# Attention, routing and experts on one core: two head units at a time on TensorE, quarter-tile work of both and then full-tile work of both

## The reference, cut to what matters

```python
h = layernorm(x) * (1 + ca) + sa
q, k, v = split(h @ Wqkv)                       # x is (2, 2048, 256); 16 heads of 64
scores = (q @ k.T) * 64 ** -0.5                 # masked to the 128 keys up to the query's own
x = x + ga * ((softmax(scores) @ v) @ Wout)
h = layernorm(x) * (1 + cb) + sb
x = x + gb * moe(h)                             # 8 experts, 2 of them per token, at most 640 tokens per expert and choice
```

## Time and profile before

| what | value |
|---|---|
| median of 3 runs | 1118.7 us (1117.24 to 1118.92) |
| the profiled execution, its own time | 1115.21 us |
| its span, first to last instruction | 1113.4 us |
| TensorE busy | 1050.8 us, 94% of the span |
| TensorE weight loads | 727.3 us, 65% |
| VectorE busy | 780.6 us, 70% |
| ScalarE busy | 660.1 us, 59% |
| GpSimd busy | 498.8 us, 45% |
| granted TensorE clock, mean | 0.986 |

### The profile page before, as it was taken

How to read it: one execution, slowest core, us unless ns; L and a number is a source line. 1 busy time by engine, 2 the same in 40 slices (tenths; PEclk the granted TensorE clock), 3 DMA queues, 4 the chain that set the end, 5 groups by cost and what they waited for, 6 DMA issues and landing times.

```text
span 1113.4 us, 28021 instructions
## 1 busy us (share of the span) xinstructions
PE 1050.8 (94%) x10746; PEld 727.3 (65%) x10746; DVE 780.6 (70%) x1745; ACT 660.1 (59%) x1930; POOL 498.8 (45%) x547
## 2 busy tenths in 40 slices
PE   7989999999999999999989866999999999999995
PEld 3456766766666666666666544668685858586765
DVE  5677767778788787776778864656676666766653
ACT  4677667567667666676655735545547372737460
POOL 2244345456365364554554653533525252435342
PEclk9999999999999999999999998999999999999998
DMA  9654111121121031122121034552535253535000
GB/s 321 121 163 158 32 21 35 44 66 38 37 75 38 9 85 26 24 69 65 43 56 58 21 112 108 101 134 79 122 111 105 95 106 115 105 116 87 15 21 10
DMA packets 140173, 87.59 MB, mean 79 GB/s; under 512 B 96756, under 2 KB 130698, under 8 KB 139916
## 3 DMA queue, kind: packets, MB, share of 16 engines
q1 hardware_dynamic: 129292, 64.29, 22.7%
q0 software_dynamic: 10752, 21.54, 7.2%
HBM read 40.02 MB, written 33.79 MB: 66 GB/s over the span
## 4 chain that ended last, share of the span: by engine, by line
PE 85%; ACT 5%; issue 4%; DVE 3%; POOL 2%; DMA 0%; SPq 0%; ACTq 0%; DVEq 0%
PE down L1838 19%; PE up L1824 17%; PE gen L666 14%; PE gen L786 8%; PE score L703 7%; PE gen L680 6%; PE gen L713 6%; PE pv L745 4%; ACT prob L1029 2%; PE pv L735 2%; DVE prob L1251 1%; ACT norm_space L1053 1%; POOL slot_inputs L1647 1%; ACT hid L1866 1%; DVE negmax L1243 1%
## 5 line engine op out<-in xcount | busy, mean ns | idle before, releaser
L1866 ACT ACTIVATE hid<-up,b1T 128x512 f16<-128x512 f32 (+2 forms) x192 | 124.5, 648 | 182.1 <-PE up L1824 180.4
L1824 PE MATMUL up<-xT,w 128*128 128x512 f16 (+2 forms) x1152 | 212.5, 345 | 11.3 <-issue 11.3
L1636 POOL TENSOR_SCALAR_AFFINE_SELECT probT_split<-probT_split 128x512 f32<-128x512 f32 x128 | 114.3, 893 | 237.7 <-ACT probT_split L1038 237.4
L1838 PE MATMUL down<-w,hid 128*128 128x256 f16 x1920 | 213.7, 274 | 3.2 <-DVE hid L1882 3.2
L1838 PEld LDWEIGHTS down<-w,hid 128*128 128x128 f16 x1920 | 188.4, 98 | 27.8 <-DVE hid L1882 3.7
L666 PE MATMUL gen<-hT,big 128*128 128x512 f16 x768 | 187.0, 383 | 2.8 <-ACT probT_split L1038 2.2
L1029 ACT ACTIVATE prob<-score,negmax 128x128 f32<-128x128 f32 x512 | 180.9, 374 | 2.8 <-DVE negmax L1243 2.8
L1824 PEld LDWEIGHTS up<-xT,w 128*128 128x128 f16 x1152 | 113.0, 98 | 105.3 <-issue 13.3
L1925 POOL DMA_INDIRECT out<-y,tail x80 | 82.5, 1031 | 206.1 <-DVE y L1910 193.2
L1882 DVE TENSOR_TENSOR hid<-hid 128x512 f16<-128x512 f32 (+2 forms) x192 | 115.2, 606 | 72.8 <-ACT hid L1867 72.4
L666 PEld LDWEIGHTS gen<-hT,big 128*128 128x128 f16 x768 | 74.9, 99 | 84.0 <-ACT probT_split L1038 4.8
(11 more groups left out here) (168 smaller groups left out, 1650.1 us busy)
## 6 DMA issues: line engine op xcount, KB each, us to landing
big<-in_L_ffn_W SPq DMA_DIRECT2D x14, 1024.0 KB, 6.5
slot_inputs<-empty_row SPq DMA_DIRECT2D x80, 129.5 KB, 2.5
out<-x SPq DMA_DIRECT2D x7, 512.0 KB
k<-k SPq DMA_DIRECT2D x48, 64.0 KB, 1.8
x<-in_L_attn_x SPq DMA_DIRECT2D x4, 512.0 KB, 4.3
x<-in_L_attn_x SPq DMA_DIRECT2D x2, 1024.0 KB, 14.5
kept<-out,tail POOLq DMA_INDIRECT x80, 3.1
out<-y,tail POOLq DMA_INDIRECT x80, 2.4
```

What stands on the lines that cost most here:

```text
L1636: pool.affine_select(out=own, in_=whole, pattern=[[0, TILES], [-1, P]], compare_op=ALU.is_gt, fill=zero, base=0, channel_multiplier=1).the ...
L1824: mm = pe.matmul(bank, w1[:, par, kd, a, ft * P:(ft + 1) * P], part_rows(e, n, xT[:, par, b * KD + kd, :]), start=(i == 0), stop=(i == 5))
L1838: mm = pe.matmul(down[n][:, s, :], hid[:, ft, a, t * P:(t + 1) * P], w2[:, par, ft, b, :], start=(i == 0), stop=(i == 3 * FT - 1))
L1866: act.activation(part_rows(e, n, hid[:, ft, 0, :]), bank, ACT.Relu, scale=1 / W_SCALE, bias=bias).then_inc(hid_hi, 1)
```

## The change

TensorE now walks the steps in pairs (i, i+1) with i even. It does `scores(i)`, `half_values` of step i, `scores(i+1)`, `half_values` of step i+1, and then the transposes and the rest of step i, and the transposes and the rest of step i+1. ACT walks the same pairs in a new order. In DVE's order three small things move: an output tile's gating goes behind the softmax work of its step, layernorm's normalising goes to step 4 of the next chunk, and the steps after it move by one. The second half of the routing statistics comes at step 11 (was 13), and what follows it comes earlier too; POOL's wait for the sent rows is replaced by waits at the two places that need it. The fourth output tile is made in step 10 (was 12). The first seven chunks are changed; the last chunk keeps its own loop.

```diff
-            OUT_TILE = {4: 0, 6: 1, 8: 2, 12: 3}
+            OUT_TILE = {4: 0, 6: 1, 8: 2, 10: 3}
-            ROUTE_AT = {"stats": (7, 13), "rstd": 14, "norm": 14, "scale": 16, "shift": 17, "token": 18, "pack": 18, "low": (18, 19)}
+            ROUTE_AT = {"stats": (7, 11), "rstd": 12, "norm": 13, "scale": 15, "shift": 16, "token": 17, "pack": 17, "low": 18}
-            LN_STATS, LN_AGGR, LN_RSTD, LN_NORM = 12, 16, 17, (18, 19)
-            LN_SCALE, LN_SHIFT, LN_PACK, LN_LOW = 4, 6, 8, 9
+            LN_STATS, LN_AGGR, LN_RSTD = 16, 18, 19
+            LN_NORM, LN_SCALE, LN_SHIFT, LN_PACK, LN_LOW = 4, 5, 7, 9, 10
...
+            def places_seen(eng, r):
+                if r < NC:
+                    at_least(eng, sent, 16 * TILES * K * (r - 1))
...
 # TensorE
-                        for i in STEPS:
-                            scores(c, i)
-                            half_values(c, i - HI_AT, (c, i - LO_AT) if i >= LO_AT else (c - 1, H - 1) if c > 0 else None)
-                            transposes(H * c + i - 2, c, ("pt", i))
-                            ...
+                        for i in STEPS[::2]:
+                            for n in (i, i + 1):
+                                scores(c, n)
+                                half_values(c, n - HI_AT, (c, n - LO_AT) if n >= LO_AT else (c - 1, H - 1) if c > 0 else None)
+                            for n in (i, i + 1):
+                                rest_of_step(c, n)
...
 # ACT
+                    def evacuations(c, i):
+                        if c > 0 and i in SECOND_V:
+                            values(c - 1, ("v", 1, SECOND_V[i]))
+                        for name in projections_at(c, i):
+                            if name[0] == "v":
+                                evacuate(c, name)
+                    def evacuate_qk(c, i):
+                        for name in projections_at(c, i):
+                            if name[0] != "v":
+                                evacuate(c, name)
...
-                        for i in STEPS:
+                        for i in STEPS[::2]:
                             exponentials(c, i - 1)
+                            if i > LAG:
+                                evacuate_qk(c, i - 1)
+                            elif c > 0:
+                                evacuate_qk(c - 1, STEPS[-1])
                             if i >= LO_AT:
                                 attn_high_part(c, i - LO_AT)
                             elif c > 0:
                                 attn_high_part(c - 1, H - 1)
+                            exponentials(c, i)
+                            attn_high_part(c, i + 1 - LO_AT)
                             copy_probT(c, i - 2)
-                            ...
+                            evacuations(c, i)
+                            evacuate_qk(c, i)
+                            copy_probT(c, i - 1)
+                            evacuations(c, i + 1)
...
 # DVE
-                            if c > 0 and i - 1 in OUT_TILE:
-                                gate_tile(c - 1, OUT_TILE[i - 1])
...
                             if c > 0 and i - 1 in OUT_TILE:
+                                gate_tile(c - 1, OUT_TILE[i - 1])
                                 add_tile(c - 1, OUT_TILE[i - 1])
...
+                                if i == LN_NORM:
+                                    ln_norm(c + 2)
...
 # POOL
-                            if c > 1 and i == pick["sent"]:
-                                pool.wait_ge(sent, 16 * TILES * K * (c - 1))
```

More of the change, by code:

```diff
@@ L402, in route_group @@
                 return (r, kind) if r < NC else (LAST, (kind[0] + "_part", r - NC))
+            def places_seen(eng, r):
+                if r < NC:
+                    at_least(eng, sent, 16 * TILES * K * (r - 1))
             def rows_seen(eng, r):
                 if r < LAST:
[L407 to L412 removed]
+                    places_seen(eng, r)
             def route_scale(eng, r):
@@ L421, in route_shift, with route_low @@
                 eng.tensor_tensor(h2[:], h2[:], modrow[:, batch(r - 1), 1:2, :].to_broadcast([P, TILES, D]), ALU.add).then_inc(r_h2, 1)
-            def route_low(eng, r, half=None):
+            def route_low(eng, r):
                 c, t0, nt, rows_out = route_round(r)
                 eng.wait_ge(r_pack_hi, r)
-                tiles = slice(t0, t0 + nt) if half is None else slice(2 * half, 2 * half + 2)
-                op = eng.tensor_tensor(rows_out[:, tiles, D:2 * D], h2[:, tiles], rows_out[:, tiles, 0:D], ALU.subtract)
-                if half != 0:
-                    op.then_inc(r_pack, 1)
+                eng.tensor_tensor(rows_out[:, t0:t0 + nt, D:2 * D], h2[:, t0:t0 + nt], rows_out[:, t0:t0 + nt, 0:D], ALU.subtract)\
+                   .then_inc(r_pack, 1)
             def load_inputs(sp):
@@ L867, in project, with rest_of_step @@
                             project_qk(cc, name)
-                    def chunk(c):
-                        for i in STEPS:
-                            scores(c, i)
-                            half_values(c, i - HI_AT, (c, i - LO_AT) if i >= LO_AT else (c - 1, H - 1) if c > 0 else None)
-                            transposes(H * c + i - 2, c, ("pt", i))
-                            if c > 0 and i in OUT_TILE:
-                                late_out(c - 1, OUT_TILE[i])
-                            if c > 0 and i in SECOND_V:
-                                project_v(c - 1, 1, [SECOND_V[i]])
-                            for name in projections_at(c, i):
-                                project(c, name)
-                            if c > 1 and i == CHOOSE_AT["logits"]:
-                                route_logits(c - 1)
-                            if c > 1 and i == CHOOSE_AT["counts"]:
-                                route_counts(c - 1)
+                    def rest_of_step(c, i):
+                        transposes(H * c + i - 2, c, ("pt", i))
+                        if c > 0 and i in OUT_TILE:
+                            late_out(c - 1, OUT_TILE[i])
+                        if c > 0 and i in SECOND_V:
+                            project_v(c - 1, 1, [SECOND_V[i]])
+                        for name in projections_at(c, i):
+                            project(c, name)
+                        if c > 1 and i == CHOOSE_AT["logits"]:
+                            route_logits(c - 1)
+                        if c > 1 and i == CHOOSE_AT["counts"]:
+                            route_counts(c - 1)
+                    def chunk(c):
+                        for i in STEPS[::2]:
[4 more added lines that the diff above has]
+                                rest_of_step(c, n)
                         if c == LAST - 1:
@@ L1199, in ln_aggregate, with ln_norm @@
                         op.then_inc(ln_mv, 1)
-                    def ln_norm(cn, tiles=range(TILES)):
+                    def ln_norm(cn):
                         if cn > 2:
                             dve.wait_ge(ln_lo, cn)
-                        norm_rows(dve, x_at(cn), xn, meanvar[0], rstd[0], ln_rstd, ln_xn, cn + 1, tiles)
+                        norm_rows(dve, x_at(cn), xn, meanvar[0], rstd[0], ln_rstd, ln_xn, cn + 1)
                     def ln_scale(cn):
@@ L1490, in chunk @@
                                     ln_aggregate(c + 3)
-                                if i in LN_NORM:
-                                    half = LN_NORM.index(i)
-                                    ln_norm(c + 3, range(2 * half, 2 * half + 2))
                         if c == LAST - 1:
@@ L1657, in chunk @@
                                 reciprocal_std(pool, meanvar[1], rstd[1], r_mv, r_var, r_rstd, c, mv_n=stats_before(c) + 2)
-                            if c > 0 and i in at["low"]:
-                                route_low(pool, c, at["low"].index(i))
+                            if c > 0 and i == at["low"]:
+                                route_low(pool, c)
                             if i == LN_LOW and c + 2 < NC:
@@ L1679, in last_chunk @@
                                 scatter(c - 1, *LAST_SENDS[i])
-                            if i == LAST_SENT:
-                                pool.wait_ge(sent, 16 * TILES * K * (c - 1))
                             if i == at["low"]:
```

21 lines of the change are left out of this document (7 added, 14 removed).

## The result

The changed kernel takes 1242.2 us (median of 4 runs, 1240.9 to 1245.6); the kernel before took 1118.0 beside it (4 runs). The ratio is 1.112, with a 95% interval of 1.110 to 1.114: 124 us slower. The forecast was 1234, with 1168 to 1268 as its range.

A forecast was written before the change was run, and what follows sets the result against it. The prediction took TensorE's own sequence, busy 94% of the span, as the bound. Its terms, 76 + 42 + 18 + 4 - 13 - 7 - 2 = 118 us on 1115.2, gave 1233, stated as 1234 us, range 1168 to 1268.

The forecast's parts named there:

- Wait A: TensorE's values of step i+1 wait for the pv bank until VectorE's `attn_low_part`: 1.36 us in 56 pairs, 76 us.
- Wait B: TensorE's second transposes wait for the gen bank until ScalarE's `probT` copy: 1.40 us in 30 pairs, 42 us.
- Wait C: TensorE's group after the second transposes waits for ScalarE to empty step i's q: 0.5 us 36 times, 18 us.
- The savings: One entry into quarter tiles and one return fewer per pair on TensorE: 0.24 us a pair, 13 us in all.
- The moves and the smaller parts: VectorE late after moved normalising and routing, 4 us; TensorE's earlier waits gone, minus 7; scatters, sent-row wait, SP's work, 0.
- chunk 6: Its last two pairs, with almost no full-tile work, were not bound by TensorE before: 2 us off Wait A.
- its own range: Forecast's narrower range, 1205 to 1262 us: Wait A at 1.1 to 1.6 us, Wait B and Wait C at 70% to all.
- Only wait A: Rival, 20%: the copy or the exponentials come earlier than laid out, so only the pv bank wait costs: 1175 us.
- The savings alone: Rival, 8%: VectorE and ScalarE empty the pv bank within `scores(i+1)`, so TensorE never stops: 1099 us.
- The clock falls too: Rival, 10%: with the stalls TensorE's granted clock falls to 0.91 in the chunks, 50 us more: 1284 us.

The follow-up runs named there:

- low part first: Changed kernel, with VectorE doing `attn_low_part` right behind `merge` in even steps instead of behind `normalise`: 1212.8 us, ratio 1.0836.
- values first: Changed kernel, with TensorE doing values(i), scores(i), scores(i+1), values(i+1) and VectorE `attn_low_part` ahead of `merge` in even steps: 1176.5 us, ratio 1.0567.
- Copy first: Changed kernel, with ScalarE doing `copy_probT(i-2)` ahead of `exponentials(i)`: 1231.3 us, ratio 1.100.
- The switch experiment: Kernel before, with the transposes between scores and values in 88 steps, one more change between quarters and full tiles in each: 1142.5 us, ratio 1.0207.
- The experiment without pairs: Kernel before, with only the change's small moves (output tile in step 10, normalising and routing steps, sent-row waits), in single steps: 1122.6 us, ratio 1.0027.
- the last pairs kernel: Changed kernel, values and `attn_low_part` first, `copy_probT` early, `exponentials(i)` cut in two, `rstd` later, gating between `row_max` and `normalise`: 1145.5 us, ratio 1.0289.
- the pairs with rstd later: Changed kernel, with the routing's `rstd` and the norm that needs it one step later (13 and 14): 1237.3 us, ratio 1.1113.

## Why the prediction was right, point by point

**Wait A** was put at 1.36 us in 56 pairs, 76 us. The timeline of pair 12 in chunk 1 shows 1.40, times 56 is 78. Read in the same way, most pairs have 1.39; pair 14 of the chunks 2 to 6 has 2.1, some pairs of chunk 0, 3 and 4 up to 2.9, the first pair of all none: about 82 us, of which some 4 are the lateness in pair 14 that is counted below with the moves. The pairs 10 and 18 have 1.11 in most chunks, for a reason that the prediction names and gives no price: in them the second scores already start 0.45 us late, after `exponentials(i-1)` on ScalarE. It said that such lateness falls into wait A, and 0.28 us of it does. (Light pairs were to take 9.2 us; pair 18 takes 9.45, and 0.17 of the difference is this.) What makes it is what was said, the order on VectorE: `low part first` took 0.7 us a pair off its row, and `values first` took the row away and 61 us with it.

**Wait B** was put at 1.40 us in 30 pairs, 42 us. It is 1.38 us in the pair shown and 1.29 in the pairs 14 and 16, in 29 pieces: 40 us at 1.38. `Copy first` shows that it comes from ScalarE's order, and that its removal would be worth 12 us and not 40. The prediction's claim about the changed kernel holds; whoever had read it as "this is what can be had back" would have been wrong.

**Wait C** was put at 0.5 us 36 times, 18 us. It is there 35 times, and short of forecast. In chunk 2, timeline of PE:

```profile
301.42 0.60 PE L710 MATMUL gen<-identf,prob 128*128 128x128 f32 x4
302.27 1.04 PE L663 MATMUL gen<-hT,big 128*128 128x512 f16 x4 [0.25 <-ACT q L1014]
```

It could go on at 301.42 + 0.44 = 301.86 and does at 302.27: 0.41 us, 14 us in all.

**The savings** of one round trip were put at 0.24 us a pair from distances between starts. The switch experiment has 0.27, 15 us over 56 pairs. The term came out 2 us short. Its upper bound, the loader's whole idle of 0.42 and 0.15, is refuted.

**The moves and the smaller parts** are the terms that were wrong. They were 4 us for VectorE's lateness, minus 7 for the waits of the earlier trace rows, and 0 for GpSimd and SyncE: -3. The experiment without pairs gives +3 for the same moves. The waits in step 4 did go. What failed is the step "the scatters, the wait for sent rows and SP's stores and transposes have a step or more of room: 0": it asked only when the scatters' own data was needed. Moving `rstd` and its norm a step took back all of the 3 us. By which way they reach TensorE stays open, as said there; the split of the keys behind the scatters had more than a microsecond to spare.

The measured terms are 78 + 40 + 14 - 15 + 3 = 120 us of 124. Each is one reading times a count, the last one from a kernel without pairs; most of the 4 us that they leave can be the lower clock (below). The prediction's were 76 + 42 + 18 + 4 - 13 - 7 - 2 = 118. The errors of C, the savings, the moves and chunk 6 (minus 4, minus 2, plus 6 and plus 2) cancel to within 2 us (for chunk 6's minus 2 no run has a number, and it is left out of the measured sum): the forecast is right in its two large terms, and lucky in the small ones. The upper end of its own range, 1262, does not come out of what it names: A at 1.6 us and B and C whole make 1248.

**The rivals.** *Only wait A* falls on the rows of B and on `copy first`. *The savings alone* falls on the first row: the pv bank was not emptied by 2.08 us. *The clock falls too*, at 50 us, is refuted in size: the granted clock over the chunks was 0.98 where it was 1.00. It did not hold throughout either. From 87 to 94 us it was 0.51, which is the lower of the two levels, 1.2 GHz instead of 2.4, and in the 13 us before, at the full clock, TensorE had been busy for 8.48 us. The chunks of the changed kernel have seven stretches at the lower level, 27 us together, where the kernel before has two, 7 us. The ones in pair 14 of the chunks 2, 3 and 5 made it 1.1, 0.4 and 0.9 us longer beyond its stall; six such stretches more are an estimated 3 to 7 us. Each begins within 1.4 us of the end of a stall of TensorE that is longer than the usual 1.4: six times 2.1 to 2.9 us, once 1.9, by the starts as for wait A. In the pairs 10 and 14 of chunk 4 stalls of 2.5 and 2.2 us were followed by none. The kernel before shows the same: right behind the 2.14 us of the earlier trace rows, which the prediction cited with the words that the clock there otherwise holds, lies one of its two stretches.

```profile
65.60:69.00 3.40, 3.39 (x31) 2.60 (x32) 3.20 (x8) 1.45 (x6) 0.08 (x1) 0.50 0.47 162
```

**Left open.** The 31.7 us of the last pairs kernel were not taken apart further (its five rows come to 39.9, less 15 for the savings is 25), nor why the pairs with rstd later gained so little in total. Two units could be held in halves of one pv bank, which would give four places and take away A. It was not tried, and no run here shows what happens when TensorE writes one half of a bank while VectorE or ScalarE empties the other.

## What to carry to other kernels

To group work on an engine that is the bound saves its switches, and takes away the distance between a buffer's last use and its next, on every engine that empties it. Before such a change, write down for each buffer when its emptier is done, in that engine's own queue, and when it is wanted again; the longer one wins, however idle that engine is on average. Here 0.27 us saved stood against 1.4 and 1.4, and the three kernels that removed or shortened one wait got back 31 of 46, 12 of 40 and 61 of 78 us, as others took its place.

## What the runs showed of the hardware that was not expected

A row of waits of TensorE is smaller than the stall. Row A's piece in the pair shown is 1.26 us and the stall by starts is 1.40, since the row counts from the modelled end of the last product (188.63 + 0.83) and not from when the next could start (0.70 later, as in an undisturbed step). Wait B has 1.21 for 1.38, C 0.25 for 0.41. Over 115 such waits (51, 29 and 35) that is an estimated 18 us which stands nowhere as idle time. It is near the 19.5 us by which TensorE's busy time rose, though the stretches of lower clock have a share in that as well.

In pair 14 of chunk 2 of the changed kernel TensorE's last record of the first values ends at 292.48, and ScalarE, which waits for these values, goes on 1.6 us after that:

```profile
294.12 0.38 ACT L1049 ACTIVATE attn<-pv 128x256 f16<-128x256 f32 x1 [1.89 <-remote]
```

With `rstd` later ScalarE goes on 0.1 us after TensorE's last record. No matmul record is missing here: the pair has its 16 and 24 products twice, and both kernels have 10746 in all. So a row of TensorE can stand 1.5 us ahead of what the engine that waits for it sees; whether the products ran later than recorded or their signal was late, the trace does not tell. The lateness was real: 0.72 us of it reached the next values, and with the lower clock behind it the pair took 12.73 us for 10.89.

The clock fell to its lower level, for 3.4 to 6.8 us, behind stalls of 1.9 to 2.9 us by TensorE's rows, and in no pair of the changed kernel whose stall was 1.4. One odd long stall in a stream of short ones cost its own length and up to a microsecond more.
